# Four-network graph kernel: 24 adding scatters of each attention stage issued in the table stage before it

## The chip, the cores and the metric

The kernel runs on one core of one Trainium2 chip. The metric is the device time of one execution in microseconds: 3377.68 us, the median of three runs between 3374.59 and 3382.0 us. A core has five engines that run side by side: TensorE (PE in the profile; its weight loads are PEld), VectorE (DVE), ScalarE (ACT), GpSimd (POOL) and SyncE (SP). Each has its own queue of instructions and is held only by waits on semaphores. Sixteen DMA engines serve transfers that SP, ACT and POOL issue.

## The reference

The input is a graph with 3125 nodes of 128 features and 50000 edges, sorted by destination. Four networks follow one another, each with a residual and a layer norm. The first is a graph transformer with two layers and is where the change lies; the second to fourth sum messages over edges, and two of them need only how often each pair (source, destination) occurs.

```python
for l in range(L):                                # L = 2
    k, q, v = typed_linear(x, ntype, Wk), ...     # 16 node types
    kT = einsum('nhd,htdo->nhto', k, Watt)        # for every node and all 32 relations
    vT = einsum('nhd,htdo->nhto', v, Wmsg)
    a = einsum('ehd,ehd->eh', kT[src,:,etype], q[dst]) * pri[:,etype].T / 4
    hag = segment_sum(vT[src,:,etype] * edge_softmax(a, dst), dst)
    x = layernorm(silu(typed_linear(hag, ntype, Wa)) * alpha + x * (1 - alpha))
```

The later networks compute sums such as `segment_sum(x[src], dst)`. The kernel does them as products with a matrix of counts (source by destination), which it has to fill first.

## The kernel before, in words

The work is a sequence of stages. Each stage is a `Stage` object with a block of instructions for every engine. When a stage closes, its semaphores are cleared and all engines meet at a barrier (line 78), so that no engine starts the next stage before the last has finished this one.

For each of the two transformer layers there are four stages.

- `project` (qkv0, qkv1) makes keys, queries and values. It also searches where each edge adds to the count matrix: `K.place` holds a cell and `K.count` a number for each of 128 edges of 392 tiles. The part before it and qkv0 have searched tiles 0 to 239 when qkv0 ends; qkv1 searches up to 391.
- `relation_table` (tab0, tab1, lines 1525 to 1641) makes kT and vT for all nodes and relations. TensorE multiplies (line 1637), DVE (line 1596) and ACT (line 1621) copy the results out of PSUM into four buffers, and SP stores each, 1024 KB, to the table in HBM (line 1572), 100 stores a stage. Before a buffer is filled again its store must have landed.
- `attention` (att0, att1, lines 1644 to 2043) works through 98 groups of 512 edges. POOL gathers table rows (line 1746, four gathers a group, 392 in all), twelve groups ahead at most; TensorE, DVE and ACT make logits, the softmax and the sums. After the last group comes a tail that joins sums over the borders of tiles: SP reads first and last rows (line 1737), TensorE transposes them (line 1825), DVE scans, and ACT writes pieces of the result (lines 1908, 1910 and, in att1, 1913). POOL scatters these to the sums (line 1753, four scatters, and in att1 line 1759, four more).
- `update` (upd0, upd1) gathers the sums and ends the layer.

**The adding scatters.** The count matrix is filled by 392 indirect DMAs from POOL (line 1515), one for each tile of 128 edges. Each adds 128 numbers of two bytes to cells of the matrix in HBM. They are shared out over the eight stages by the table `COUNTS` (lines 27 and 28), written by hand: 24 in qkv0, 128 in tab0, 24 in att0, 20 in upd0, and the same again for the second layer. `count_tiles` (line 1509) issues a stage's range. A batch has eight scatters; from the eighth batch on, POOL waits until the batch seven before has landed. `await_tiles` (line 1519) waits at the stage's end for all of them. The filled matrix is first read after upd1.

**POOL's order in a table stage:** 25 scatters of query rows (line 1550), four gathers (line 1555), `count_tiles` (line 1557), the wait for the first two kinds, the copy of the opening rows (line 1560) and the wait for it, then `await_tiles`.

**POOL's order in an attention stage:** the 392 gathers, `count_tiles` (line 1748), the wait for the tail's reads and for ACT's pieces, line 1753, in att1 also line 1759, the wait for these, then `await_tiles`.

Of the kernel before, what the change touches and what calls it, by code (L numbers as in the profile page):

```python
# [21 lines left out]
TILES = EP // P  # L22
# [1 line left out]
TURNS, BLOCKS = TILES // STREAMS, STREAMS // BLOCK  # L24
EARLY_TURNS = 13
SEEKS = (range(13, 30), range(30, TILES // SEEK))
COUNTS = {"qkv0": range(0, 24), "tab0": range(24, 152), "att0": range(152, 176), "upd0": range(176, 196),
          "qkv1": range(196, 220), "tab1": range(220, 348), "att1": range(348, 372), "upd1": range(372, TILES)}
EXT = N + 1
AW = -(-(EXT + STREAMS) // 32) * 32  # L30
NTYPES, RELS, HEADS, HS, LAYERS = 16, 32, 8, 16, 2
# [2453 lines left out]
def build(nc, D, out):  # L2485
# [21 lines left out]
    with ExitStack() as stack:  # L2507
        def sb(name, shape, dt=F32, st=stack):
            return st.enter_context(nc.sbuf_tensor(name, shape, dt))
# [16 lines left out]
        with ExitStack() as inner:  # L2526
# [12 lines left out]
            for l in range(LAYERS):  # L2539
                wk, wv = (sb(f"{x}{l}", [P, RELS, QUAD], st=table) for x in ("wk", "wv"))  # L2540
                rows = sb(f"qkv_rows{l}", [P, NT, 3 * P], st=table)
                key, value = (sb(f"{x}{l}", [P, NP], st=table) for x in ("key", "value"))
                project(nc, K, D, l, hx, w, wk, wv, rows, (key, value), SEEKS[l], COUNTS[f"qkv{l}"])
                relation_table(nc, K, D, f"tab{l}", wk, wv, key, value, rows, COUNTS[f"tab{l}"], l == 0)
                table.close()
                attention(nc, K, D, f"att{l}", l, a, COUNTS[f"att{l}"])
                table = ExitStack()
                w = sb("w1", [P, NTYPES, 3 * P], st=table) if l == 0 else None
                update(nc, K, D, l, hx, l == LAYERS - 1, w, COUNTS[f"upd{l}"])
            nc.clear_and_free_semaphores([K.weights])  # L2550
# [75 lines left out]
```

## Time and profile before

| what | value |
|---|---|
| median of the runs (lowest, highest) | 3377.68 us (3374.59, 3382.0) |
| span of the profiled execution, first to last instruction | 3371.0 us; its own device time is not given apart from the runs |
| POOL busy | 2145.1 us, 64% of the span |
| PE, DVE, ACT busy | 2414.2, 1869.8, 1218.8 us |
| adding scatters, line 1515 | 392, 619.0 us busy, 1579 ns each |
| table gathers, line 1746 | 784, 797.1 us busy, 1017 ns each |
| tab0, att0, upd0 start (SP's first instruction) | 267.03, 567.94, 1145.56 us |
| att1, upd1 start | 1636.99, 2226.02 us |

Busy time is when an engine executes; for a DMA issued by POOL it is the issue, not the transfer. A share of the whole span mixes stages with different limits, so what counts here is each stage by itself: which engine or queue finishes last before the barrier. In the timeline a row gives the start, the duration, the engine, the line, the operation, and in brackets how long the engine stood idle before it and what released it.

### The profile page before, as it was taken

The numbers are of one execution on the slowest core, as the hardware profiler recorded it, in microseconds if no ns is written. First come the engines' busy times: TensorE is split into PE (matmuls) and PEld (weight loads), VectorE is DVE, ScalarE is ACT, GpSimd is POOL, SyncE is SP. The second block draws the span as 40 slices with busy tenths as digits, with TensorE's granted clock in tenths as the row PEclk, the third lists the DMA queues.
The fourth block names the chain that finished last, engine by engine and source line by source line (L and its number), as shares of the span: only waits on it lengthen the run. The fifth ranks groups of instructions, "written<-read, shape, count | busy, mean of one in ns | idle before, by whom it ended". The sixth has DMA issues, their size and how long they took to land. (4 is left out here: it accounts for less than half of the span.)

```text
span 3371.0 us, 43562 instructions
## 1 busy us (share of the span) xinstructions
PE 2414.2 (72%) x12333; PEld 1764.7 (52%) x12333; DVE 1869.8 (55%) x4323; ACT 1218.8 (36%) x2988; POOL 2145.1 (64%) x1938
## 2 busy tenths in 40 slices
PE   1647995666666377999466666644686999997787
PEld 1435663555555245666355555522574666664676
DVE  6743443555556267444355555534435888886444
ACT  0114442222223273444122222335444555554444
POOL 4556885777777767888577777865404777775100
PEclk9965555788888687555587787767797999998798
DMA  9998998889987556999788988747554666663653
GB/s 296 260 351 312 389 386 276 245 261 270 269 266 215 127 103 201 387 388 361 225 257 251 271 266 255 197 87 140 141 192 126 194 193 194 193 195 104 222 190 124
DMA packets 679422, 790.51 MB, mean 235 GB/s; under 512 B 141399, under 2 KB 563102, under 8 KB 651434
## 3 DMA queue, kind: packets, MB, share of 16 engines
q1 hardware_dynamic: 321380, 498.68, 43.7%
q0 software_dynamic: 118784, 156.95, 19.9%
q10 hardware_dynamic: 239062, 132.59, 13.2%
q8 instruction: 84, 1.38, 0.2%
q14 instruction: 112, 0.92, 0.1%
HBM read 379.46 MB, written 408.59 MB: 234 GB/s over the span
## 5 line engine op out<-in xcount | busy, mean ns | idle before, releaser
L1746 POOL DMA_INDIRECT att_rows<-table,kvrow x784 | 797.1, 1017 | 291.7 <-issue 232.8
L1515 POOL DMA_INDIRECT matrix<-count,place x392 | 619.0, 1579 | 128.8 <-issue 119.4
L2339 POOL DMA_INDIRECT msg_rows<-rows,msg_src x392 | 384.1, 980 | 260.9 <-DMA msg_src<-in_src_pt 141.8
L1596 DVE COPY tab_part<-tab_bank 128x512 f32<-128x512 f32 x400 | 257.3, 686 | 316.8 <-DMA table<-tab_part 277.7
L1803 PE MATMUL att_po<-att_message,att_mate 128*128 128x264 f32 (+1 forms) x1568 | 397.2, 408 | 11.8 <-ACT att_out L1871 5.5
L1637 PE MATMUL tab_bank<-wk,tab_kv 32*128 32x256 f32 x1600 | 364.3, 695 | 35.3 <-DVE tab_part L1596 23.5
L1929 DVE TENSOR_TENSOR att_prod<-att_rows,att_pq 128x512 f32<-128x512 f32 x196 | 134.5, 686 | 425.5 <-DMA att_rows<-table,kvrow 425.3
L1772 PE MATMUL att_pq<-a,att_mate 128*128 128x128 f32 x1152 | 207.1, 337 | 215.3 <-DVE att_prod L1929 215.3
L1803 PEld LDWEIGHTS att_po<-att_message,att_mate 128*128 128x128 f32 x1568 | 304.9, 236 | 69.2 <-DVE att_message L1980 26.7
L1621 ACT ACTIVATE tab_part<-tab_bank 128x512 f32<-128x512 f32 x400 | 221.6, 594 | 322.6 <-DMA table<-tab_part 301.6
L1637 PE MATMUL tab_bank<-wv,tab_kv 32*128 32x256 f32 x1600 | 332.5, 616 | 0.0
L1772 PEld LDWEIGHTS att_pq<-a,att_mate 128*128 128x128 f32 x1152 | 186.8, 243 | 244.6 <-issue 240.0
L1871 ACT ACTIVATE att_out<-att_po 128x136 f32<-128x136 f32 (+1 forms) x784 | 224.0, 337 | 240.7 <-PE att_po L1803 235.0
L1637 PEld LDWEIGHTS tab_bank<-wk,tab_kv 32*128 32x128 f32 x1600 | 203.8, 301 | 186.7 <-DVE tab_part L1596 160.1
L1637 PEld LDWEIGHTS tab_bank<-wv,tab_kv 32*128 32x128 f32 x1600 | 234.8, 321 | 12.3
L2396 ACT ACTIVATE msg_sc<-msg_rows,msg_edge 128x128 f32<-128x128 f32 x392 | 125.4, 391 | 244.7 <-DMA msg_rows<-rows,msg_src 240.1
L1772 PE MATMUL att_pq<-att_query,att_mate 128*128 128x128 f32 x416 | 80.5, 356 | 155.6 <-DVE att_prod L1929 93.1
L2380 PE MATMUL msg_pm<-msg_prod,down 128*128 128x512 f32 x392 | 184.5, 593 | 0.0
L1921 DVE TENSOR_TENSOR att_mate<-att_rank,rank_own 128x512 f32<-128x512 uint8 x196 | 134.0, 684 | 56.4 <-DMA att_rank<-rank 56.4
L1772 PEld LDWEIGHTS att_pq<-att_query,att_mate 128*128 128x128 f32 x416 | 72.3, 259 | 168.3 <-issue 135.1
L1844 ACT ACTIVATE att_weight<-att_less 128x128 f32<-128x128 f32 (+1 forms) x50 | 15.5, 309 | 393.9 <-DVE att_less L1954 393.9
L2450 DVE TENSOR_TENSOR msg_prod<-msg_pr,msg_un 128x512 f32<-128x512 f32 x196 | 134.2, 685 | 36.5 <-PE msg_pr L2359 34.9
(435 smaller groups left out, 4513.6 us busy)
## 6 DMA issues: line engine op xcount, KB each, us to landing
table<-tab_part SPq DMA_DIRECT2D x200, 1024.0 KB
att_sums<-att_out ACTq DMA_DIRECT2D x196, 272.0 KB
gcn_cells<-matrix SPq DMA_DIRECT2D x50, 800.0 KB
a<-query_rows SPq DMA_DIRECT2D x144, 256.0 KB
query_rows<-a SPq DMA_DIRECT2D x16, 1568.0 KB
att_message<-in_ea_rows SPq DMA_DIRECT2D x98, 256.0 KB, 4.1
sums<-att_out ACTq DMA_DIRECT2D x98, 256.0 KB, 5.5
msg_hidden<-hidden SPq DMA_DIRECT2D x196, 128.0 KB
```

Of the source, the lines that this page charges most:

```text
L1515: nc.gpsimd.indirect_dma_start(D.matrix, bass.IndirectOffsetOnAxis(ap=K.place[:, col:col + 1], axis=0), K.count[:, col:col + 1], None, com ...
L1596: nc.vector.tensor_copy(quad_columns(c // 2, c % 2), bank[c // 2 % 2 * 4 + c % 2][:, :].rearrange("p (n r d) -> p n r d", n=2, d=QUAD)).th ...
L1621: nc.scalar.activation(quad_columns(c // 2, 2 + c % 2), bank[c // 2 % 2 * 4 + 2 + c % 2][:, :].rearrange("p (n r d) -> p n r d", n=2, d=QUAD),
L1637: last = nc.tensor.matmul(bank[q % 2 * 4 + quad][:, k * (W // 2):(k + 1) * (W // 2)], kv[u][rows, k, :], w[rows, q * 8:q * 8 + 8, :].rearr ...
L1746: nc.gpsimd.indirect_dma_start(rows[g % RR][:, j, :], None, D.table, bass.IndirectOffsetOnAxis(ap=K.kvrow[:, t:t + 1], axis=0)).then_inc(r ...
L1772: last = nc.tensor.matmul(pq[g % 2][:, j * P:(j + 1) * P], mate[g % RS][:, j, :], query[g % RQ][:, j, :], start=True, stop=True)
L1803: nc.tensor.matmul(po[j][:, 0:w], mate[h % RS][:, j, :], message[h % RM][:, j, 0:w], start=True, stop=True).then_inc(summed, 1)
L1871: nc.scalar.activation(out[k][:, j, 0:w], po[j][:, 0:w], ACT.Copy).then_inc(copied, 1)
L1929: nc.vector.tensor_tensor(prod[g % 2][:, :, :], rows[g % RR][:, :, 0:P], pq[g % 2][:, :].rearrange("p (j d) -> p j d", j=J), ALU.mult).the ...
L2339: nc.gpsimd.indirect_dma_start(rows[g % RR][:, j, :], None, D.rows, bass.IndirectOffsetOnAxis(ap=src[:, t:t + 1], axis=0)).then_inc(rows_i ...
L2380: nc.tensor.matmul(pm[n][:, :], down[n][:, :], prod[n][:, :], start=True, stop=True).then_inc(mapped, 1)
L2450: nc.vector.tensor_tensor(prod[n][:, :], pr[n][:, :], un[g % 2][n][:, :], ALU.mult).then_inc(multiplied, 1)
```

## The change

The table of ranges gives the 24 tiles of each attention stage to the table stage before it. tab0 issues tiles 24 to 175 and tab1 tiles 220 to 371, 152 each; the ranges of att0 and att1 are empty, so that `count_tiles` and `await_tiles` issue and wait for nothing there. All else is as it was.

```diff
-COUNTS = {"qkv0": range(0, 24), "tab0": range(24, 152), "att0": range(152, 176), "upd0": range(176, 196),
-          "qkv1": range(196, 220), "tab1": range(220, 348), "att1": range(348, 372), "upd1": range(372, TILES)}
+COUNTS = {"qkv0": range(0, 24), "tab0": range(24, 176), "att0": range(176, 176), "upd0": range(176, 196),
+          "qkv1": range(196, 220), "tab1": range(220, 372), "att1": range(372, 372), "upd1": range(372, TILES)}
```

## Rows read from the trace of the kernel before

**Rows 1.** The page: the span.

```profile
span 3371.0 us, 43562 instructions
```

**Rows 2.** Stretches: engines in the order PE, PEld, DVE, ACT, POOL; clock, DMA, GB/s.

```profile
400.00:500.00 100.00, 98.91 (x592) 67.50 (x590) 46.88 (x73) 43.14 (x92) 83.79 (x54) 0.50 1.09 386
543.00:553.00 10.00, 0.00 (x0) 0.00 (x0) 2.16 (x3) 1.04 (x2) 0.74 (x1) 0.50 0.84 288
...
559.00:568.00 9.00, 0.00 (x0) 0.00 (x0) 0.00 (x0) 0.06 (x1) 0.00 (x0) 0.50 0.00 0
568.00:600.00 32.00, 13.42 (x53) 11.75 (x54) 11.66 (x18) 1.22 (x1) 24.04 (x25) 0.50 0.94 259
```

**Rows 3.** Waits, first table stage: who, for what, us in total, times, longest.

```profile
ACT tab_part L1621 <- DMA table<-tab_part: 138.6, 88, 2.2
...
POOL matrix L1515 <- issue: 39.0, 128, 0.3
```

**Rows 4.** Timeline, first table stage: start us, us, engine, line, operation, idle before.

```profile
305.15 1.61 POOL L1515 DMA_INDIRECT matrix<-count,place  x1 [0.30 <-issue]
...
541.30 1.55 POOL L1515 DMA_INDIRECT matrix<-count,place  x1 [0.30 <-issue]
...
542.29 1.45 POOL L1560 DMA_DIRECT2D query_rows<-tab_opens  x1
...
567.94 0.33 SPq L1722 DMA_DIRECT2D att_rank<-rank  x1
```

**Rows 5.** The DMA queue of the scatters, 553 to 568 us.

```profile
q0 software_dynamic: 921, 0.02, 14.1%
```

**Rows 6.** Stretches of the two attention loops, the gathers of line 1746 alone.

```profile
568.60:1083.00 514.40, 395.20 (x392) 0.80 0.88 258
1637.70:2159.00 521.30, 401.95 (x392) 0.78 0.86 254
```

**Rows 7.** Timeline, end of the first attention stage.

```profile
1122.76 0.20 ACT L1910 ACTIVATE att_message<-att_po 98x32 f32<-98x32 f32 x1 [0.25 <-PE att_po L1833]
...
1132.10 0.99 POOL L1753 DMA_INDIRECT att_sums<-att_message,first_end  x1 [0.30 <-issue]
...
1135.91 0.95 POOL L1753 DMA_INDIRECT att_sums<-att_message,first_end  x1 [0.30 <-issue]
...
1145.56 0.84 SPq L721 DMA_DIRECT2D upd_w<-in_L_gnn_Wa  x1
```

**Rows 8.** Timeline, end of the second attention stage.

```profile
2203.09 0.20 ACT L1910 ACTIVATE att_message<-att_po 98x32 f32<-98x32 f32 x1 [0.26 <-PE att_po L1833]
...
2204.85 0.60 ACT L1913 ACTIVATE att_message<-att_po 98x512 f32<-98x512 f32 x1 [1.57 <-PE att_po L1833]
...
2207.25 0.98 POOL L1753 DMA_INDIRECT att_sums<-att_message,first_end  x1 [0.30 <-issue]
```

**Rows 9.** Waits, first attention tail: who, for what, us, times, longest.

```profile
PE att_pq L1825 <- DMA att_rows<-att_sums: 8.0, 1, 8.0
```

**Rows 10.** Landing of the fixing scatters of line 1753, from issue.

```profile
DMA to landing us min/median/max: 2.2/2.3/2.3
```

**Rows 11.** The scatters of the first attention tail, and their landing from issue.

```profile
L1515 POOL DMA_INDIRECT matrix<-count,place x24: 1561/1563/3911, 1083.3 to 1130.2; - x24
...
DMA to landing us min/median/max: 2.9/3.0/4.5
```

**Rows 12.** Timeline, the first projection ends and the first table stage starts.

```profile
265.84 0.31 ACT L652 ACTIVATE value<-qkv_acc 128x128 f32<-128x128 f32 x1
...
267.03 0.37 SPq L1566 DMA_DIRECT2D query_nodes<-qkv_rows  x1
```

**Rows 13.** Timeline, second table stage, the same columns.

```profile
1607.72 1.47 POOL L1560 DMA_DIRECT2D query_rows<-tab_opens  x1
...
1636.99 0.32 SPq L1722 DMA_DIRECT2D att_rank<-rank  x1
```

**Rows 14.** The scatters' DMA queue in the first table stage, 400 to 543 us.

```profile
q0 software_dynamic: 11089, 0.02, 14.1%
```

## The prediction

> **What bounds the kernel now.** The page comes first, for the span of 3371.0 us that everything is measured against [rows 1]. The result's median is 3377.68 us, 6.7 us more than that span; the profiled execution's own time is not given apart, so I make the sum on the span and add its difference to the median. The busy shares of the whole span decide nothing here, since the change touches two pairs of stages. So I went on to the stretches, the waits, and the timeline at the four places where such a stage ends.
>
> *Table stages.* While the table is written, DMA moves 386 GB/s at a share of 1.09, and TensorE has its lower clock, 0.50 of full speed or 1.2 GHz [rows 2]. The evacuations wait for table writes 88 times, 138.6 us in total, while POOL waits for nothing but its own 0.3 us of issue between scatters [rows 3]. So the writes bound the inner part, and POOL runs beside them at a pace of its own. That pace: 128 scatters start between 305.15 and 541.30, which is 236.15 / 127 = 1.859 us each [rows 4]. What the reader is to see is how close the two finish. POOL ends its last scatter at 542.85 and issues the copy of line 1560 at 542.29; the writes run on at 288 GB/s to 553, small packets until 559 [rows 5], then nothing moves for 9 us [rows 2], and attention's first instruction is issued at 567.94 [rows 4]. POOL is only some 10 us ahead of the writes, not 45.
>
> *Attention stages.* The loop issues 392 gathers in 514.4 and 521.3 us [rows 6]; the moved scatters stand behind the last gather on POOL, so the loop does not meet them. In the tail, 24 scatters run from 1083.3 to 1130.2. The work that they cover ends sooner: ScalarE finishes the second fixed-up piece at 1122.76 + 0.20 = 1122.96, but the fixing scatter of line 1753, which waits for it, starts only at 1132.10, directly behind the last adding scatter [rows 7]. In the second attention stage that pair is 2203.29 and 2207.25 [rows 8]. There POOL's queue sets the end, and there is the whole of the gain.
>
> **The change, part by part.**
>
> *Removed: 24 scatters from each attention tail.* Line 1753 then waits for ScalarE plus a 0.3 us issue. First stage: 1132.10 - 1123.26 = **8.8 us**. Second: 2207.25 - 2203.59 = 3.7 us; the fourth of its scatters would end some 5 us later at 2208.6, after the third fixed-up piece at 2204.85 + 0.60 = 2205.45 [rows 8], so nothing new holds line 1759. The gain is **12.5 us**. Could the tail itself shorten? The engines in it don't wait for POOL, but TensorE waits 8.0 us for the read of the edge rows [rows 9]; a fixing scatter lands in 2.3 us [rows 10]. If all the difference were the scatters' traffic, 5.7 us a stage would be gained; if the queue does not matter, nothing. I take nothing, since 24 scatters are a trickle beside the stores there, and keep 11.4 us for the range. In the other direction, nothing in the tail is put behind anything, so I see no loss.
>
> *Added: the same 24 in each table stage, on POOL, behind the 128 and ahead of lines 1558 to 1561.* Issue: 24 x 1.859 = 44.6 us. What is queued behind them on POOL is the copy of line 1560, its wait, and the wait for all scatters; every other engine is held at the stage's end by the barrier, and so is attention's start, with its 392 gathers. First stage: line 1560 moves from 542.29 to 586.9. It lands about 2.8 us after its start (2.3 us for a fixing scatter [rows 10], plus 0.5 us since its own issue takes 1.45 and not 0.95), at 589.7; the last adding scatter starts at 585.9 and lands 3.0 us later [rows 11], before it. Then comes the way out of the stage. No row shows it with a quiet queue in this stage. From below it is 0.9 us: after the first projection ScalarE ends at 266.15 and SP issues at 267.03 [rows 12]. From above it is 8.9 us: from silence at 559 to 567.94 [rows 2]. The nearest row is the first attention's end, where POOL was also last: 1135.91 + 2.3 = 1138.2 to 1145.56 is 7.4 us [rows 7]. I take 8.1 us, between the two that have POOL last. Attention then starts at 597.8: 29.9 us later than 567.94. Second stage: line 1560 moves from 1607.72 to 1652.3, lands at 1655.1, attention starts at 1663.2 instead of 1636.99 [rows 13]: 26.2 us. Together **56.1 us**. So of 2 x 44.6 us only 33 are hidden, by the last table writes and by the scatters' backlog; that cover is then used up.
>
> *Costed at nothing.* The table writes: they end near 553 either way, under POOL's new end. SP's queue: it has no instruction of the scatters, and its next one is behind the barrier. The landing waits inside the scatters (a batch of 8 must wait for the batch 7 before it, 56 x 1.859 = 104 us earlier) are long met. The places that the scatters need, 152 to 175 and 348 to 371, are computed in the projection stages, which search to 239 and 391. TensorE's clock: attention's first 32 us have 0.50 already [rows 2], and a longer pause cannot take it below its lower level; the gathers' pace sets that stretch anyway.
>
> *A rule against the rows.* One packet of the scatters' queue costs 14.1% x 16 engines x 143 us / 11089 packets = 29 ns, and a scatter has 11089 x 1.859 / 143 = 144 packets [rows 14]. 24 scatters are 3456 packets, 6.3 us of all sixteen engines. Of the moved ones only the 5 issued before 553 meet writes at all, and the 1.3 us that they take end under POOL. The Trainium skill, page "DMA: Bandwidth & Descriptors", section "Queues, rings and completion order", says that each engine takes turns between the queues that have work, a packet at a time. By that rule, were the writes the last thing in the stage, small packets would lengthen it by up to 6.3 us twice, 12.6 us, and the sum would be about zero; by the rows it is POOL's issue that ends last.
>
> *Sum:* +56.1 - 12.5 = +43.6 us. Span 3414.6; against the median 3377.68 + 43.6 = **3421 us**.
>
> **The rivals.**
>
> *The lag stays (6%).* After 553 the scatters' queue still had 921 packets to move [rows 5], 6.4 scatters; the last scatter's end and attention's start are 25.1 us apart. If each stage keeps this lag behind POOL, nothing is hidden: 89.2 - 12.5 = +76.7, 3454 us. Against: 921 packets in 6 us is 0.94 us a scatter or less, twice as fast as POOL issues, so the backlog is gone long before 587.
>
> *A cheap way out (6%).* If most of the quiet 9 us is waiting that overlaps POOL's end, only 0.9 us follow the landing: 2 x 7.2 us less, +29.2, 3407 us. Against: the 7.4 us at attention's end.
>
> *Scatters go faster once the writes stop: not slower (4%).* This needs 1.859 us to be the loaded queue's pace and not POOL's. With T us for a moved scatter the two stages cost 48 T - 33, and the net is 48 T - 45.6: no loss below T = 0.95, within 0.2% below T = 1.09. At the backlog's pace of 0.94 for all 24 it is -0.5 us; if the first five keep 1.859, T is 1.13 and the net +8.7. I price it at -0.5 us, 3377 us. Against: beside the much lighter attention tail (24 scatters, median 1.563 us [rows 11]) they take no less than beside the writes (1.55 [rows 4]), so it is POOL's own time.
>
> *Faster (2%):* the above and shorter tails together, -0.5 - 11.4, 3366 us. *The change does not do what it says:* the counts are plain ranges and an empty one issues and awaits nothing; I give it no chance.
>
> **How the numbers follow.** 82% for the forecast. Its own bounds: way out 7.4 or 8.9 us (2 x 0.8), tails up to 11.4 less, the two gather loops differ by 521.3 - 514.4 = 6.9 us for the same work, and the runs by 3374.59 to 3382.0. That gives 3406 to 3433; I reach down to 3404 for the cheap way out and up to 3442 for part of the lag. Some 0.2%, 6.8 us, is what a measurement of this kernel can tell from no change. Slower: 82 + 6 + 6 = 94%. Same: 4%. Faster: 2%.
>
> **What would show it.** In the changed profile: 152 scatters in each table stage at 1.86 us; POOL's last one in the first ending near 587.5; attention starting near 598 and, the second time, near 1663 + 30 - 9 = 1684; line 1753 following line 1910 by 0.3 to 0.5 us in both tails; no line 1515 in either. Wrong would be: scatters under 1.1 us after 553, attention's start above 605 or below 590, or a tail more than 3 us shorter before line 1910.

## The result and the profile after

The changed kernel takes 3431.35 us (median of four runs, 3430.31 to 3434.68) against 3377.41 us (four runs): the ratio is 1.0158 with a 95% interval of 1.014 to 1.0175, some 54 us slower; the forecast was 43.6. In another set of runs the same pair gave 1.0152 (1.0138 to 1.0167). The span of the profiled execution is 3432.9 us; its device time was 3434.68.

Two lines of the changed kernel's page, its span and its adding scatters. They are 392 as before, so nothing was added, only moved:

```profile
span 3432.9 us, 43558 instructions
...
L1515 POOL DMA_INDIRECT matrix<-count,place x392 | 611.1, 1559 | 128.5 <-issue 119.9
```

The changed kernel's timeline where the first table stage ends, which answers to [rows 4] (start, duration, engine, line, operation; in brackets the idle time before it and what ended it):

```profile
585.75 1.55 POOL L1515 DMA_INDIRECT matrix<-count,place  x1 [0.30 <-issue]
...
586.73 1.46 POOL L1560 DMA_DIRECT2D query_rows<-tab_opens  x1
...
597.07 0.33 SPq L1722 DMA_DIRECT2D att_rank<-rank  x1
```

POOL's last adding scatter starts at 585.75 (forecast 585.9), the copy of line 1560 at 586.73 (586.9), and attention at 597.07 (597.8). The stretches of the changed kernel, with the columns of [rows 2], show what covered the scatters before and what no longer does:

```profile
400.00:500.00 100.00, 98.81 (x591) 67.18 (x585) 47.59 (x74) 43.72 (x92) 83.54 (x55) 0.50 1.09 385
...
568.00:586.00 18.00, 0.00 (x0) 0.00 (x0) 0.00 (x0) 0.00 (x0) 14.95 (x11) 0.50 0.20 0
...
590.00:597.00 7.00, 0.00 (x0) 0.00 (x0) 0.00 (x0) 0.00 (x0) 0.00 (x0) 0.50 0.00 0
...
598.00:630.00 32.00, 14.05 (x57) 12.49 (x57) 12.39 (x21) 0.35 (x1) 24.61 (x25) 0.55 0.93 260
```

The writes go at 385 GB/s, as before. From 568 to 586 nothing but POOL works, on 11 scatters, and the DMA share is 0.20. The stage ends with POOL's queue alone, and after the pause attention's first 32 us have a granted clock of 0.55, no lower than the 0.50 of before [rows 2].

The changed kernel's timeline at the end of the first attention stage, which answers to [rows 7]:

```profile
1162.97 0.20 ACT L1910 ACTIVATE att_message<-att_po 98x32 f32<-98x32 f32 x1 [0.26 <-PE att_po L1833]
...
1164.03 0.98 POOL L1753 DMA_INDIRECT att_sums<-att_message,first_end  x1 [42.15 <-ACT att_message L1910]
...
1167.84 0.95 POOL L1753 DMA_INDIRECT att_sums<-att_message,first_end  x1 [0.31 <-issue]
...
1180.41 0.84 SPq L721 DMA_DIRECT2D upd_w<-in_L_gnn_Wa  x1
```

The fixing scatter now waits for ScalarE (42.15 us idle, released by line 1910) and starts 0.86 us after ScalarE's end; before it was 9.14 us. But from the last fixing scatter to the next stage it is 1180.41 - 1167.84 = 12.6 us, where [rows 7] have 9.65. The queue instructions at the end of the block name the difference. They are in the view of one source line, for POOL's DRAIN at the end of a stage's block (min, median and max duration in ns, then its start). The kernel before, at the end of the first attention stage and of the second:

```profile
L75 POOLq DRAIN  x1: 5937/5937/5937, 1138.3 to 1138.3; - x1
...
L75 POOLq DRAIN  x1: 6263/6263/6263, 2218.5 to 2218.5; - x1
```

The changed kernel at the same two places:

```profile
L75 POOLq DRAIN  x1: 8882/8882/8882, 1170.3 to 1170.3; - x1
...
L75 POOLq DRAIN  x1: 9208/9208/9208, 2276.4 to 2276.4; - x1
```

The DRAIN has grown by 2.9 us in each, and it lies between the last scatter and the next stage.

The same view shows what holds the end of a table stage. The kernel before, first table stage, SP and POOL:

```profile
L75 SPq DRAIN  x1: 7/7/7, 554.3 to 554.3; - x1
...
L75 POOLq DRAIN  x1: 4381/4381/4381, 562.8 to 562.8; - x1
```

The changed kernel, the same place:

```profile
L75 POOLq DRAIN  x1: 5687/5687/5687, 590.6 to 590.6; - x1
```

SP has left its wait for the last table write at 554.3. POOL leaves its waits for its own DMAs only at 562.8, its DRAIN takes 4.4 us, and 0.8 us after that attention starts. So already before the change the stage's end hung on the landings of POOL's queue. The quiet 9 us of [rows 2] are 3.8 us in which POOL still waits for landings that no packet shows, and 5.2 us of way out. In the changed kernel the same order stands 28 us later, with a DRAIN 1.3 us longer.

Stage lengths, from one stage's first instruction to the next one's (SP's first instruction for the table, attention and update stages, the first memset of POOL for the projections), worked out from the timelines:

| stage | before | changed | difference | forecast |
|---|---|---|---|---|
| table, first layer | 300.9 | 330.8 | +29.9 | +29.9 |
| attention, first layer | 577.6 | 583.3 | +5.7 | -8.8 |
| update and projection between | 185.7 | 188.1 | +2.4 | 0 |
| table, second layer | 305.8 | 331.3 | +25.5 | +26.2 |
| attention, second layer | 589.0 | 587.0 | -2.0 | -3.7 |

In the first attention stage the tail's 8.3 us of gain stand against 2.9 of DRAIN and a gather loop that was 9.8 us longer than the 513.4 before; the first experiment is about that loop. The prediction had the second start of attention near 1684; it was at 1699.84, since the first attention stage grew instead of shrinking (14.5 us) and the stages between grew by 2.4.

### The profile page after: what moved, and what is told of

It reads as the page before. It is cut to its first block and busy times, and to the rows that moved or that the text cites. A ratio compares the mean times of both kernels' runs of the same rounds, so it can differ in the third digit from the quotient of the medians.

```text
span 3432.9 us, 43558 instructions
## 1 busy us (share of the span) xinstructions
PE 2425.1 (71%) x12333; PEld 1775.1 (52%) x12333; DVE 1869.4 (54%) x4323; ACT 1217.4 (35%) x2988; POOL 2150.9 (63%) x1938
## 5 line engine op out<-in xcount | busy, mean ns | idle before, releaser
L1746 POOL DMA_INDIRECT att_rows<-table,kvrow x784 | 806.1, 1028 | 257.6 <-issue 232.0
L1515 POOL DMA_INDIRECT matrix<-count,place x392 | 611.1, 1559 | 128.5 <-issue 119.9
L1803 PE MATMUL att_po<-att_message,att_mate 128*128 128x264 f32 (+1 forms) x1568 | 404.9, 414 | 10.1 <-ACT att_out L1871 5.7
L1772 PE MATMUL att_pq<-a,att_mate 128*128 128x128 f32 x1152 | 215.0, 346 | 224.5 <-DVE att_prod L1929 224.3
L1772 PEld LDWEIGHTS att_pq<-a,att_mate 128*128 128x128 f32 x1152 | 194.3, 252 | 254.8 <-issue 249.3
```

What stands on the lines that cost most here:

```text
L1515: nc.gpsimd.indirect_dma_start(D.matrix, bass.IndirectOffsetOnAxis(ap=K.place[:, col:col + 1], axis=0), K.count[:, col:col + 1], None, com ...
L1746: nc.gpsimd.indirect_dma_start(rows[g % RR][:, j, :], None, D.table, bass.IndirectOffsetOnAxis(ap=K.kvrow[:, t:t + 1], axis=0)).then_inc(r ...
L1772: last = nc.tensor.matmul(pq[g % 2][:, j * P:(j + 1) * P], mate[g % RS][:, j, :], query[g % RQ][:, j, :], start=True, stop=True)
L1803: nc.tensor.matmul(po[j][:, 0:w], mate[h % RS][:, j, :], message[h % RM][:, j, 0:w], start=True, stop=True).then_inc(summed, 1)
```

## The experiments

Each kernel is the one before with another table of ranges; all else is the same. The diffs show only the entries of the table that differ from the kernel before. Ratios are to the kernel before on the same chip.

**The kernel before, again.** No edit. Its expectation:

> The kernel of before, unchanged, for the spread of what is compared. In the change's profile the first attention loop (first to last gather of line 1746) took 523.2 us where the profile of before had 513.4, although nothing was changed in it. Theory A (spread): the loop's length varies from execution to execution by some 10 us, so this profile shows it anywhere between 510 and 525 us. Theory B (the change slows the loop): here it is 513 +-2 us again. The time is that of before within 0.2% either way.

Ratio 1.0006 (0.9993 to 1.002). Its first attention loop took 520.8 us instead of 513.4, its second 516.3 instead of 520.2. The stretch that holds the 392 gathers of the first loop, in this kernel's profile (POOL's busy time in line 1746, then clock, DMA share and GB/s):

```profile
567.50:1090.00 522.50, 402.61 (x392) 0.76 0.86 254
```

Over the thirteen profiles of this study the first loop lies between 513.4 and 523.2 us and the second between 514.8 and 520.4, and the kernels that leave a loop's scatters alone lie among those that don't. Theory A holds and theory B falls: a difference of 9.8 us is within the spread of single executions, and the 61.9 us between the two spans overstate the change by some 8 us. A small effect on the loop is not excluded: with nothing moved in its layer the first loop took 513.4, 515.2 and 520.8 us, with all 24 moved 518.0 to 523.2 in four profiles; the second loop shows none (516.3 to 520.2 against 515.6 to 519.5).

**The change again, and its two halves.**

First layer only:

```diff
-"tab0": range(24, 152), "att0": range(152, 176)
+"tab0": range(24, 176), "att0": range(176, 176)
```

Second layer only:

```diff
-"tab1": range(220, 348), "att1": range(348, 372)
+"tab1": range(220, 372), "att1": range(372, 372)
```

> Only the first layer's 24 scatters are moved. By the sum of the prediction it costs 29.9 us in the table stage and gains 8.8 in the attention stage: +21 us, ratio 1.0062. By the change's profile the attention stage gains less, since POOL's DRAIN at the end of its block takes 8.9 us instead of 5.9 and the fixing scatter starts 0.9 us behind ScalarE: +25 us, 1.0074. If the change also slows the loop by 10 us: +35 us, 1.0104. The DRAIN is expected at 8.9 us in the first attention stage and 6.3 us in the second.

> The changed kernel once more, beside the parts below on one chip. By the stage lengths seen so far it costs 30.2 us in the first table stage and 25.6 in the second and gains 5.4 and 0.3 us in the attention stages: +50 us, ratio 1.0149. If the parts hide something outside these stages, it stays at 1.0158 or above.

> The first layer alone gave 1.0105 where its stage lengths give 30.2 - 5.4 = 24.8 us, 1.0074. If that was the spread of four runs, it is 1.0074 +-0.0015 now. If something that the profile of one execution does not show costs 10 us, it is 1.010 again.

> Only the second layer's 24 scatters are moved: 25.6 us in the table stage, 0.3 us gained in the attention stage, ratio 1.0075. By the prediction's sum it would be 26.2 - 3.7 = 22.5 us, 1.0067. Its trace should have the second attention stage's DRAIN at 9.2 us and the first's at 5.9 us. With the first layer alone it adds up to the whole change within 5 us; if it does not, the two parts are not independent.

First layer only: 1.0105 (1.0087 to 1.0123) in four runs, then 1.007 (1.0048 to 1.0092) in five more. Second layer only: 1.0064 (1.0045 to 1.0083). The whole: 1.0152 (1.0138 to 1.0167), where the stage lengths gave 1.0149. The two intervals of the first layer overlap only at their edges; the stage lengths of both profiles agree with each other (331.4 and 331.0 us for the table, 578.1 and 576.7 for attention), so the 12 us between the two ratios are not in the moved stages. The medians lie closer together than the ratios do, 31.0 and 28.0 us above those of before; nothing was found but the spread between runs. The second set adds up: 0.70 + 0.64 = 1.34% against 1.52%, 6 us apart where 5 were allowed, and the three intervals are some 5 to 7 us to each side; by the medians it is 28.0 + 21.6 = 49.6 us against 50.5. The DRAINs with the second layer alone are 5.93 us in the first attention stage and 9.20 in the second, as expected.

**Six and three.** Only as many scatters are moved as the tails need to lose.

```diff
-"tab0": range(24, 152), "att0": range(152, 176)
+"tab0": range(24, 158), "att0": range(158, 176)
-"tab1": range(220, 348), "att1": range(348, 372)
+"tab1": range(220, 351), "att1": range(351, 372)
```

> Six scatters are moved from the first attention stage and three from the second, each to the table stage before it; that is as many as the tail needs to get rid of. Theory slack (the prediction's: 14.7 and 18.3 us of POOL's issue are hidden in the table stages): nothing is paid there, gain 12 us less what the DRAIN changes, ratio 0.9965 to 0.9975. Rival backlog: the scatters' queue is behind when the table writes end and moves one scatter in 0.9 us, so each moved scatter delays the last landing and with it the stage's end by 0.9 us though POOL's issue is hidden: 8.1 us paid, gain 4 us, 0.9988. In its trace: attention starts 0 to 1 us later after the table stage's start (slack) or 5 to 6 us later (backlog).

0.9981 (0.9967 to 0.9995): this version is faster than both kernels, if by little. The fixing scatters start 0.9 us behind ScalarE in both stages, as with all 24 moved. The table stages are 302.3 and 306.4 us, 1.4 and 0.7 us longer than before. That is neither nothing nor the rival's 5.6 and 2.8. In the first, POOL left its waits for landings 0.8 us later for six scatters, not 5.6, and its DRAIN took 0.5 us more: the backlog does not add up.

**Other stages.** The table stages keep 128; six scatters go to the first projection, three from the second attention stage end up in the first update.

```diff
-"qkv0": range(0, 24), "tab0": range(24, 152), "att0": range(152, 176), "upd0": range(176, 196),
-"qkv1": range(196, 220), "tab1": range(220, 348), "att1": range(348, 372)
+"qkv0": range(0, 30), "tab0": range(30, 158), "att0": range(158, 176), "upd0": range(176, 199),
+"qkv1": range(199, 223), "tab1": range(223, 351), "att1": range(351, 372)
```

> The table stages keep 128 scatters each. Six of the first attention stage's go to the first projection stage, where POOL's block ends 11 us before ScalarE's, and three of the second's are taken up by the first update stage, where POOL's ends 6 us before the barrier; the tiles between move along. Theory: all of the attention tails' gain is kept and nothing is paid, 11 to 12.5 us faster than before, ratio 0.9963 to 0.9967. Rival: the projection stage is held by its gathers behind the six scatters (11 us later), then the gain of the first layer is lost there: 2 to 4 us faster, 0.999.

> The version that pays nothing in the table stages, once more, since its first interval was 0.9972 to 0.9995. By stage lengths it gains 8.2 + 0.5 us in the first attention stage and 3.1 + 0.2 in the second: ratio 0.9964. If the first interval's middle is right, 0.9984.

0.9984 (0.9972 to 0.9995) and 0.9986 (0.9975 to 0.9998): faster than before, by some 5 us (7.4 us both times by the medians), and no better than six and three. The stage lengths had promised 12, which both intervals exclude (at most 9.4 and 8.4 us). In the profiles the table stages are as before (301.0 and 301.0; 305.5 and 305.0) and the tails are as planned. The place was not free: the part up to the first table stage and the part from the first update to the second table stage are 1.2 and 0.9 us longer than the mean of the other eleven profiles. Nor is the promised gain there in every execution: the 9.14 us by which the fixing scatter of before trails ScalarE are 5.40 in another profile with the first layer unchanged. With both counted some 8 us are left, which the intervals allow.

**One left.** The first theory on the DRAIN: one scatter of each attention stage stays.

```diff
-"tab0": range(24, 152), "att0": range(152, 176)
+"tab0": range(24, 175), "att0": range(175, 176)
-"tab1": range(220, 348), "att1": range(348, 372)
+"tab1": range(220, 371), "att1": range(371, 372)
```

> As the change, but each attention stage keeps one scatter, so that a scatter still stands between the gathers and the fixing scatters. Theory one (POOL's DRAIN costs 0.082 us for each DMA that POOL has not yet retired, and a scatter makes it retire some 60 gathers): the DRAIN is 5.94 - 23 x 0.082 = 4.1 us and 4.4 us instead of 8.9 and 9.2, so with 151 scatters in the tables instead of 152 it is 9.7 + 3.7 = 13 us faster than the change. Theory two (the DRAIN is long because POOL stands idle 42 us before the fixing scatters): it stays at 8.8 to 9.2 us, and only the 3.7 us are gained.

1.0128 (1.0108 to 1.0148), which lies between the two forecasts and decides neither. The DRAIN does. POOL's DRAIN at the end of the first attention stage of this kernel:

```profile
L75 POOLq DRAIN  x1: 8958/8958/8958, 1160.9 to 1160.9; - x1
```

Theory one falls: a scatter between the gathers and the fixing scatters does not shorten the DRAIN, it lengthens it by 0.08 us, as one more DMA. The level is the one that theory two forecast (in the second attention stage 9.28 us), with 39.7 and 42.9 us of idling; the next run bears on its cause. The table stage with 151 scatters took 328.7 us, 2.1 us less than with 152.

**Fewer in the tables, and the step of the DRAIN.** 12 and 6 scatters of the table stages and 12 and 20 of the attention stages are left out altogether.

```diff
-"tab0": range(24, 152), "att0": range(152, 176)
+"tab0": range(24, 140), "att0": range(152, 164)
-"tab1": range(220, 348), "att1": range(348, 372)
+"tab1": range(220, 342), "att1": range(348, 352)
```

> 36 adding scatters and 18 more are left out, so the count matrix is incomplete: the first table stage issues 116 (12 left out), the second 122 (6 left out), the first attention stage 12 (12 left out), the second 4 (20 left out). Only stage lengths are read. Table: if the writes' own end holds the stage, 12 fewer scatters shorten it by nothing; if the scatters' last landing and POOL's DRAIN behind it hold it, 12 fewer bring it from 300.9 to some 290 us and 6 fewer from 305.6 to some 298 us. DRAIN: its time has followed the number of POOL's DMAs in the stage, 0.082 us each, with a drop of 4.9 us somewhere between 401 and 414; here the first attention stage has 408 and the second 404. If the count alone decides, each shows either 9.5 to 9.9 us (drop still ahead) or 4.6 to 5.0 us (drop passed); if it is the kind of instruction, both are long.

POOL's DRAIN at the end of its first attention stage:

```profile
L75 POOLq DRAIN  x1: 4957/4957/4957, 1130.4 to 1130.4; - x1
```

The attention stages, with 408 and 404 DMAs, have 4.96 and 4.63 us, so both lie behind the drop. In the second, POOL stood idle this long before its first fixing scatter (what released it, us in total, times):

```profile
  ACT att_message L1910: 37.3, 1
```

So some 37 us of idling do not by themselves make the DRAIN long, and the first stage, with 15.4 us of idling, follows the same 0.082 us for each DMA. But what sets the place of the drop is not shown: it lies between 401 and 404 DMAs, which is also between one and four adding scatters, and between 37.3 and 39.7 us of idling. The runs move the three together.

The table stages are 297.4 and 304.3 us, 3.5 and 1.5 us shorter. Neither theory had that: 0 if the writes' end holds the stage, 11 and 8 if the last landing does and moves with POOL's issue. The end of the first table stage, which here starts at 268.28:

```profile
L75 SPq DRAIN  x1: 7/7/7, 555.0 to 555.0; - x1
...
L75 POOLq DRAIN  x1: 4054/4054/4054, 560.9 to 560.9; - x1
```

SP is done with the writes 286.7 us into the stage, against 287.3 before, so 12 scatters fewer moved the end of the writes by 0.6 us. POOL left its waits at 292.6 instead of 295.8 us, and its DRAIN was 0.3 us shorter; that is the 3.5. The landings of POOL's queue hold the stage's end with 116 scatters as with 128. They do not follow POOL's issue, which ended 22.3 us earlier here, but come 6 to 8 us behind the writes (10 with six more) and move by 0.26 us for each scatter left out and 0.14 for each of the six added. What spaces them so stays open. A delay of the writes by the scatters' packets is not it: by [rows 14] 12 scatters are 3.1 us of all sixteen engines, but the writes ended only 0.6 us sooner without them, and with 152 scatters sooner than with 128, not later (286.9). The Trainium skill (page "DMA: Bandwidth & Descriptors", section "Queues, rings and completion order") says that engines take turns between queues, a packet at a time; no run here shows the turns, nor a delay of that size.

**Twelve each.** Half of the change.

```diff
-"tab0": range(24, 152), "att0": range(152, 176)
+"tab0": range(24, 164), "att0": range(164, 176)
-"tab1": range(220, 348), "att1": range(348, 372)
+"tab1": range(220, 360), "att1": range(360, 372)
```

> Half of the change: 12 scatters of each attention stage are moved. Only stage lengths are read. If a table stage hides what the prediction said (14.7 us of POOL's issue in the first, 18.3 in the second) and then pays 1.86 us for each scatter, the first is 7.6 us longer than before, 308.5 us, and the second 4.0 us longer, 309.6 us. If instead the cost runs evenly from 0 to 24 scatters, they are 15 and 13 us longer. DRAIN by the count of POOL's DMAs (408 and 412 in the attention stages): 5.0 and 5.3 us.

One execution, profiled. The timeline at the end of its first table stage:

```profile
563.57 1.45 POOL L1560 DMA_DIRECT2D query_rows<-tab_opens  x1
...
572.91 0.33 SPq L1722 DMA_DIRECT2D att_rank<-rank  x1
```

With attention's first instruction at 572.91, 4.97 us after that of before, the table stages took 307.5 and 309.3 us (forecast 308.5 and 309.6), not the 316 and 319 of an even cost; the DRAINs in the attention stages 4.96 and 5.28 us (5.0 and 5.3). The cost of a moved scatter has a knee. The first few cost 0.22 us each in both stages (six and three), those from 12 to 24 cost 1.94 and 1.83. The two lines cross near ten and eleven moved scatters, where the sum had eight and ten. The whole kernel took 3379.23 us against 3381.76 of before, one run each, too few to tell a gain.

All of it in one table. "Writes" is when SP leaves its wait for the last write and "landed" when POOL leaves its last wait for its own DMAs (the starts of their DRAINs), both in us from the stage's start; 0.8 us behind the DRAIN the next stage starts.

| scatters | stage | writes | landed | DRAIN | length |
|---|---|---|---|---|---|
| 116 | tab0 | 286.7 | 292.6 | 4.05 | 297.4 |
| 128 (before) | tab0 | 287.3 | 295.8 | 4.38 | 300.9 |
| 134 | tab0 | 286.9 | 296.6 | 4.87 | 302.3 |
| 140 | tab0 | 287.0 | 302.1 | 4.71 | 307.5 |
| 151 | tab0 | 286.8 | 322.3 | 5.61 | 328.7 |
| 152 (changed) | tab0 | 286.9 | 324.3 | 5.69 | 330.8 |
| 122 | tab1 | 291.5 | 299.0 | 4.54 | 304.3 |
| 128 (before) | tab1 | 292.1 | 300.6 | 4.38 | 305.8 |
| 131 | tab1 | 291.9 | 301.0 | 4.63 | 306.4 |
| 140 | tab1 | 292.7 | 303.9 | 4.71 | 309.3 |
| 151 | tab1 | 292.3 | 323.3 | 5.61 | 329.7 |
| 152 (changed) | tab1 | 291.7 | 324.8 | 5.69 | 331.3 |

## Why the prediction was right, point by point, and where it was short

The forecast was 3421 us in a range from 3404 to 3442; 3431.35 lies inside it, 10 us above the forecast.

*What ends last in a table stage:* right. The sum hid 14.7 and 18.3 of the 44.6 us of POOL's issue [rows 4, 13]; the stages grew by 29.9 and 25.5 us against 29.9 and 26.2. Twelve each puts the knee within two scatters of where the sum put it. What the sum did not see is which landing ended last before the change: POOL's own, at 562.8, not the silence at 559. That the first stage's 29.9 is met to 0.1 us is luck in part. From line 1560's start to the next stage it is 10.3 us, where the sum had 10.9: POOL's wait was over 3.7 us after that start (forecast 2.8), and 6.6 us followed (forecast 8.1), of which the DRAIN took 5.7. Against that, line 1560 itself started 0.6 us later into the stage than forecast.

*The gain in the tails:* 8.3 and 3.1 us against 8.8 and 3.7. The mechanism was right; the wake-up is 0.9 us behind ScalarE, and I had only the 0.3 us that separate two scatters in a row. The size is that of one execution: in the three profiles with the first attention stage unchanged the fixing scatter trails ScalarE by 9.14, 9.13 and 5.40 us, in the four with the second unchanged by 2.93 to 3.98. The tails themselves did not shorten: TensorE's wait for the edge rows is 7.6 us, against 8.0 [rows 9]. From the waits of the first attention tail of the changed kernel (total us, times, longest):

```profile
PE att_pq L1825 <- DMA att_rows<-att_sums: 7.6, 1, 7.6
...
POOL att_sums L1753 <- ACT att_message L1910: 42.1, 1, 42.1
```

*The step that failed:* "In the other direction, nothing in the tail is put behind anything, so I see no loss." The way out of the attention stage, which the sum held constant, grew by 2.9 us in each: DRAIN from 5.94 to 8.88 us and from 6.26 to 9.21. With it, and the measured 55.4 and 11.4 us in place of 56.1 and 12.5, the sum is 55.4 - 11.4 + 5.9 = +49.9 us instead of +43.6. The measured +54 (47 to 59 by the interval) and, the second time, 1.0152 or +51 agree with that; the 4 us that the first measurement lies above it are within its interval and were not traced further. The queue instructions at the blocks' ends in the trace before show DRAINs of up to 26.7 us, which I had not read; they do not show that this one would jump.

*The rivals:* the backlog did not stay behind POOL's new end (attention started 9.8 us after POOL's last scatter ended, not 25.1), though before the change its landings did hold the stage. The way out was not cheap, and scatters did not go faster in the quiet queue: they started 1.86 us apart to the end. The costs at nothing held: the writes kept 385 GB/s and in the first table stage their end stayed within 0.8 us, and the granted clock in attention's first 32 us did not fall. The delay of the writes by the scatters' packets, 6.3 us a stage if the writes held the end, was not seen in any run; the writes held the end in none of them.

## What to carry to other kernels

An engine that is ahead of the bound of a stage has a small, countable slack; moving work under a cover is worth it up to that slack, and the rest is paid in full: here some ten scatters at 0.22 us each and the rest at about 1.9. Equally, a tail gains only until the next thing is late: six of the 24 gave all of the first stage's gain, three that of the second. So move the smaller of the two numbers, not the whole lot: six and three were 0.2% faster where 24 and 24 were 1.6% slower.

## What the runs showed of the hardware that was not expected

In the attention stages POOL's DRAIN at the end of the block goes by the number of DMAs that POOL has issued in the stage, although all of them have landed when it starts. It repeats to 0.01 us over thirteen profiles.

| POOL's DMAs in the attention stage | 396 | 397 | 400 | 401 | 404 | 408 | 412 | 414 | 420 | 421 | 424 |
|---|---|---|---|---|---|---|---|---|---|---|---|
| DRAIN, us | 8.88 | 8.96 | 9.21 | 9.28 | 4.63 | 4.96 | 5.28 | 5.45 | 5.94 | 6.02 | 6.26 |

Each DMA adds 0.082 us, and between 401 and 404 the time falls by 4.9 us, the worth of 60. In the first update stage 60 DMAs have 4.95 us and 63 have 5.20. In the table stages the step is 0.082 us too, from 116 to 122, from 128 to 134 and from 140 to 152 scatters, but it falls by 0.65 us, the worth of eight, between 122 and 128 and again between 134 and 140. So neither the size nor the place of a fall carries over from one stage to another. In blocks of other kinds the count does not give the time: two blocks of the kernel before with 38 and 380 DMAs of POOL have 19.3 and 19.7 us. What POOL does in this time no run shows.
